# Where the low part of x is made, and when the expert units are loaded, in a convolution-and-experts kernel

## The reference

```
k = conv(x, w1, padding 6, dilation 2);  k = relu(k + b1)
k = relu(batch_norm(conv(k, w2) + b2));  attn = softmax(k, axis=1)
out = sum over p of patch_p(x) * attn[:, p]          # 49 taps
x = x + out
t = t + experts(ln(t)),  top 2 of 8 experts, weights from a softmax over mean(t) @ Wr
```

## Time and profile before

| | us |
|---|---|
| median of 3 runs | 980.85 (979.34 to 983.98) |
| the profiled execution | 980.27, of which the span of the trace is 978.5 |
| PE busy | 909.7 (93%) |
| DVE busy | 699.5 (71%) |
| ACT busy | 528.8 (54%) |
| POOL busy | 141.8 (14%) |
| 16 unit loads xs<-in_ew, 512 KB each | median 4.3 from issue to landing |

### The profile page before, as it was taken

The page is one execution under the profiler, slowest core; times in us unless marked ns, Lnnn a source line. Parts: engine busy times, 40 slices in busy tenths (PEclk is TensorE's granted clock), DMA queues, the critical chain, the costliest instruction groups (busy, mean ns, idle before and its releaser), DMA issues. The chain is left out here.

```text
span 978.5 us, 19546 instructions
## 1 busy us (share of the span) xinstructions
PE 909.7 (93%) x7659; PEld 755.1 (77%) x7659; DVE 699.5 (71%) x1824; ACT 528.8 (54%) x981; POOL 141.8 (14%) x164
## 2 busy tenths in 40 slices
PE   3787999999999969999999947999999999999997
PEld 2776888888888858888999934777777777777776
DVE  3797567477658619836579866878877887788777
ACT  4796343434444211133445438686867777687851
POOL 1100110000010200200113220111221212112122
PEclk9999999999999998989999968999999999999999
DMA  9721311132200144720558446354255335424211
GB/s 215 217 61 52 95 49 50 50 91 62 63 26 25 45 138 131 200 50 2 132 150 220 133 121 164 90 128 96 64 152 110 66 85 159 98 50 98 66 33 49
DMA packets 134826, 95.01 MB, mean 97 GB/s; under 512 B 63579, under 2 KB 129516, under 8 KB 134636
## 3 DMA queue, kind: packets, MB, share of 16 engines
q1 hardware_dynamic: 134734, 93.77, 37.5%
HBM read 54.91 MB, written 29.40 MB: 86 GB/s over the span
## 5 line engine op out<-in xcount | busy, mean ns | idle before, releaser
L1316 PE MATMUL pM<-V,U 128*128 128x264 f16 (+3 forms) x2352 | 294.6, 283 | 0.0
L1316 PEld LDWEIGHTS pM<-V,U 128*128 128x128 f16 x2352 | 230.5, 99 | 44.6
L1824 ACT ACTIVATE gf<-pH,b1c,sc 128x384 f32<-128x384 f32 x192 | 127.7, 669 | 83.8 <-issue 67.2
L2131 PE MATMUL pH<-xT,w1h 128*128 128x384 f16 x768 | 157.9, 329 | 5.8 <-DMA xT<-xs 3.4
L2145 PE MATMUL pY<-w2h,gh 128*128 128x256 f16 x576 | 157.0, 273 | 0.3 <-DVE w2l L1989 0.3
L2145 PE MATMUL pY<-w2h,gl 128*128 128x256 f16 x576 | 157.0, 273 | 0.0
L2145 PE MATMUL pY<-w2l,gh 128*128 128x256 f16 x576 | 157.0, 273 | 0.0
L1997 DVE SCALAR_TENSOR_TENSOR gl<-gf,sc,gh 128x384 f16<-128x384 f32 x192 | 112.1, 620 | 50.2 <-ACT gh L1815 50.2
L2131 PEld LDWEIGHTS pH<-xT,w1h 128*128 128x128 f16 x768 | 75.0, 99 | 55.6 <-ACT gf L1824 4.8
L1815 ACT ACTIVATE gh<-gf,sc 128x384 f16<-128x384 f32 x192 | 115.4, 616 | 0.0
L775 ACT CAST V<-pV 128x336 f16<-128x336 f32 x96 | 42.0, 437 | 133.3 <-PE pV L1287 133.3
(11 more groups left out here) (252 smaller groups left out, 1357.2 us busy)
## 6 DMA issues: line engine op xcount, KB each, us to landing
xa<-in_xt SPq DMA_DIRECT2D x16, 576.0 KB, 6.4
xs_scratch<-xs SPq DMA_DIRECT2D x16, 576.0 KB, 4.3
tk<-t_scratch SPq DMA_DIRECT2D x24, 384.0 KB, 3.8
out<-o SPq DMA_DIRECT2D x23, 384.0 KB, 2.9
xs<-in_ew SPq DMA_DIRECT2D x16, 512.0 KB, 4.3
U<-xs_scratch SPq DMA_DIRECT2D x16, 480.0 KB, 4.7
V<-in_w1g SPq DMA_DIRECT2D x6, 784.0 KB, 8.4
w1r<-in_ew SPq DMA_DIRECT2D x8, 512.0 KB, 4.3
```

What stands on the lines that cost most here:

```text
L1316: return nc.tensor.matmul(out[:, :, first:end], U[:, k, hi_u, piece, :], V[:, b % 2, hi_v, k, c, :, first + TILES * d:end + TILES * d], st ...
L1824: nc.scalar.activation(gf[:, (JB * m + j) % GBUFS, :], pH[:, (JB * m + j) % HBUFS, 0:CN], ACT.Gelu, bias=b1c[:, j // FB, j % FB:j % FB + 1 ...
L2131: last = nc.tensor.matmul(pH[:, (JB * m + j) % HBUFS, 0:CN], w[:, k, c, f * P:(f + 1) * P], xT[:, s, x, c, :], start=(i == 0), stop=(i == ...
```

## The change

Two edits. The low part of x, a subtraction of 96x1536 elements for each of the 16 images, is no longer VectorE's but GpSimd's, which has it in its program among its reciprocal roots. And SyncE issues the loads of the first three expert units before the store and loads of the norm's numbers, the attention maps and the spread table, the other fourteen where all stood; the slots of the last batch in which VectorE takes units begin at 1 instead of 0, and slots 7 and 8 have three units each instead of two.

```
-STAGES, UNITS_SLOT = 3, {0: 1, 1: 2, 2: 2, 3: 2, 4: 2, 5: 2, 6: 2, 7: 2, 8: 2}
+STAGES, UNITS_SLOT = 3, {1: 1, 2: 2, 3: 2, 4: 2, 5: 2, 6: 2, 7: 3, 8: 3}
@@ block.sync, behind the loops over the batches
+            def load_units(units):
+                for u in units:
+                    if u >= STAGES:
+                        sp.wait_ge(unit_taken, u - STAGES + 1)
+                    src, dst = unit(u)
+                    sp.dma_start(dst, src).then_inc(unit_loaded[u % STAGES], 16)
+
+            sp.wait_ge(v_turned, V_TURNS * IMGS)
+            for s in range(2):
+                sp.wait_ge(xs_stored[s], 16 * IMGS // 2)
+            load_units(range(STAGES))
             sp.wait_ge(ln_taken, 2)
             sp.dma_start(ln_d.rearrange("w (r p) -> r w p", p=TT), ln_rows).then_inc(ln_stored, 16)
...
             sp.wait_ge(m_ready, NP * (B - 1) + G_FREE)
             sp.dma_start(G[:, :, :], spread_d).then_inc(g_loaded, 16)
-            for s in range(2):
-                sp.wait_ge(xs_stored[s], 16 * IMGS // 2)
-            sp.wait_ge(v_turned, V_TURNS * IMGS)
-            for u in range(UNITS):
-                if u >= STAGES:
-                    sp.wait_ge(unit_taken, u - STAGES + 1)
-                src, dst = unit(u)
-                sp.dma_start(dst, src).then_inc(unit_loaded[u % STAGES], 16)
+            load_units(range(STAGES, UNITS))
@@ block.gpsimd
+            def x_low(n):
+                pool.wait_ge(xhi_split, n + 1)
+                nc.gpsimd.tensor_tensor(xs[:, n % 2, :, 1, :], xa[:, n % XBUFS], xs[:, n % 2, :, 0, :],
+                                        ALU.subtract).then_inc(xlo_split, 1)
+
             rsqrt(0)
             rsqrt(1)
+            x_low(0)
             rsqrt(2)
             pool.wait_ge(bn_step, 1)
             pool.wait_ge(size_step, 6)
             nc.gpsimd.tensor_tensor(bnp[:, 6:7], bnp[:, 5:6], mhalf[0:TAPS, 0:1], ALU.pow).then_inc(bn_rstd, 1)
+            x_low(1)
             for n in range(3, IMGS):
                 rsqrt(n)
+                if n <= BI:
+                    x_low(n - 1)
+                if n >= BI:
+                    x_low(n)
@@ block.vector
-            def x_low(n):
-                dve.wait_ge(xhi_split, n + 1)
-                tt(xs[:, n % 2, :, 1, :], xa[:, n % XBUFS], xs[:, n % 2, :, 0, :], ALU.subtract).then_inc(xlo_split, 1)
-
...
                     u_low(U_PAIR * pair + j)
-                    if pair + j == 0:
-                        x_low(0)
...
-                x_low(pair + 1)
...
-                    if k in SPLIT_SLOT and BI * (b + 1) + SPLIT_SLOT[k] < IMGS:
-                        x_low(BI * (b + 1) + SPLIT_SLOT[k])
```

## The result

The changed kernel takes 983.77 us in the median (980.57 to 990.81) beside 979.10 us of the kernel before: ratio 1.0042, interval [1.0026, 1.0058], 4.1 us more (2.5 to 5.7).

What follows compares the result with a forecast made beforehand. Setup was taken as bound by engines handing work round, the convolution by TensorE. Loads and table -8.8, setup +8.2, convolution +2.4 gave +1.8 on 980.3, so 982.1 us, range 974 to 990.

Steps and rivals of the forecast that it cites:

- The stall: Last batch: TensorE idles 8.62 us before logits while VectorE awaits the first expert unit; early loads save 11.0 us.
- The table: Last batch, slots 7 and 8: three units each delay VectorE's spread subtraction; TensorE's fourth spread waits, +2.2 us (0 to 3.3).
- GpSimd's operation: Each image's low-part subtraction, 96x1536: 3.45 us on GpSimd, range 2.9 to 4.0, against VectorE's 1.75.
- Convolution: Images 5, 6, 7, 10 and 14: GpSimd's low part comes late for TensorE's turn, +2.4 us in all.
- Image 0: Setup: GpSimd finishes the low part later, so TensorE's turn starts at 27.3 instead of 25.59, +1.7 us.
- Image 1: Setup: GpSimd's low part stops VectorE's tap-table multiply, delaying TensorE by 0.7 us; 3.4 if L1158 is caught instead.
- Images 2 and 3: Setup: GpSimd's low part stops VectorE's tap-table multiply, for which TensorE waits; +2.5 and +2.2 us.
- Rival 1: Setup: GpSimd does not stop the tap-table multiply; sum -5.5, 974.8 us. Chance 18%, 22% with a faster GpSimd operation.
- Clock: Setup, images 2 and 3: idle TensorE may drop to its lower clock, 1.6 us each; one taken, +1.6 (0 to 3.2).
- Image 4: Setup: GpSimd delivers the low part at 96.2, ahead of TensorE's former start at 96.80; -0.5 us.
- Rival 2: Low parts everywhere: mixed form slower on GpSimd, 990.1 us at 4.0 us each; chance 20%, 28% with image 1's other collision.
- Rival 3: Last batch: loads not early enough or late slots swallow the gain, first part gives about nothing; 991 us, chance 4%.

Runs made afterwards that it cites:

- pool_plus_1us: Changed kernel plus a 6-column GpSimd power operation ahead of the low parts of images 5 to 15; 1.0139 of the kernel before, +13.6 us.
- behind_bn: Changed kernel, but GpSimd starts image 1's low part only after the six steps of bn_scales; 1.0018 of the kernel before, +1.8 us.
- behind_taps: Changed kernel, but GpSimd starts the low parts of images 2 and 3 only after their pair's tap table is scaled; 0.9960 of the kernel before, -3.9 us.
- low_only: Changed kernel with unit loads and slot table put back as before, low parts still on GpSimd; 1.0097 of the kernel before, +9.5 us.
- table_in_psum: Changed kernel with the tap table copied once to PSUM and read there by VectorE's multiply; 0.9959 of the kernel before, -4.0 us.
- loads_only: Changed kernel with every low part back on VectorE, early loads and new slot table kept; 0.9932 of the kernel before, -6.7 us.

## Why the prediction was right in its sum and wrong in its steps

The forecast of 982.1 us and "within 0.5%" held: +1.8 forecast, +4.1 measured, though the interval reaches to 0.58% and the loss itself is clear of zero. That it held is in part luck: the setup lost 13.2 us instead of 8.2, and the convolution nothing instead of 2.4.

- **The stall** (-11.0). Right: between the same two logits -11.2 us in the trace, VectorE's wait for the first unit gone, TensorE 30.00 of 30 us busy.
- **The table** (+2.2). Right place and mechanism, three takes ahead of the fourth spread; the size was low. In the trace of the changed kernel the wait is 1.66 us, and 3.4 are lost over the spreads; the pairs of variants have 2.4 to 3.9. The 21 matmuls behind the wait took 4.01 us instead of 2.60, a low clock that the term left out.
- **GpSimd's operation** (3.45 us). 3.10: (3096 - 195)/1530 = 1.90 ns a column, not 2.13. The mixed form is cheaper than the f32 one. By the Trainium skill, GPSIMD Engine Reference, section 3.1, the estimate was 3.4 us; it is for f32, and for this form the measurement decides against both.
- **Convolution** (+2.4). Wrong, from that term: 0.08 + 3.10 fits into the 3.27 us with 0.1 to spare. `pool_plus_1us` shows that the mechanism was right: by its waits, little more than 0.1 us added to the operation would have begun to cost.
- **Image 0** (+1.7). Right: 1.4 us in every trace with GpSimd there, in line with 3.10 - 1.75. Another 0.4 us lie ahead of it and are the kernel's start. The matmuls behind it ran at the low clock (3.18 us for eight), 1.2 us more than before up to the mark of image 1; but variants with image 0 on VectorE have up to 2.4 more, so this is not shown to be the change's doing.
- **Image 1** (+0.7). This step failed. I left the other collision, L1158's, out of the sum and gave it 8%, together with low clocks at both later images; both occurred. It cost 2.9 us instead of 0.7; `behind_bn`, without it, is 2.8 us shorter in that stretch of the trace and 2.3 in the ratio. When an outcome hangs on which of two operations starts first within 0.1 us, a chance near one half was due: of the five traces with this order left open it was caught in two (the changed kernel, `behind_taps`) and free in three (`low_only`, `table_in_psum`, `pool_plus_1us`). The collision that I did forecast here, GpSimd's end against the multiply, is real but smaller: 0.58 us for 0.34 in `low_only`.
- **Images 2 and 3** (+2.5, +2.2). Rival 1 is out: the multiply is stopped, 2.37 us instead of 0.34. The direct price was 2.03 each.
- **Clock** (+1.6, one of two falls). Too low: both came, 1.57 us at image 2 and 2.3 at image 3. Low stretches of the clock ahead of the first convolution matmul sum to 21.7 us after, 5.1 before. At images 0, 1, 2 and 3 the matmuls behind a wait of 2.5 to 2.9 us ran at the low level; at image 1 they had done so before the change too. The stretches between the waits are longer by 1.2, 0.3, 1.6 and 2.3 us behind images 0 to 3, 5.3 in all, and for the two multiplies' part, 3.9, this agrees with the ratios (8.0 - 4.1).
- **Image 4** (-0.5). -0.8.

Setup in the trace: 0.4 for the start + 1.4 + 2.9 + 2 x 2.03 + 5.3 for these stretches - 0.8 = 13.2, but for rounding, against 8.2. Rival 2's mechanism is out, at 3.10 us; what it named beside it (image 1's collision and cold starts at both later images, +6.1) is what happened, and the sum stayed at +4.1 mainly because the convolution cost nothing. Rival 3 is out: `loads_only` gains 6.7 us.

The Trainium skill, SBUF — State Buffer, section "SBUF: two separate sides", has the pair of ports shared by VectorE and GpSimd as an exclusive lock for the whole instruction, held by whichever starts first. The traces agree: 2.37 us for 0.34, 3.14 for 0.24, GpSimd's 4.05 for 3.10 where VectorE was first, and 0.24 where VectorE was 0.08 us ahead. What tells the two scalings from the one-column operations that ran free, no run here separates.

## What to carry to other kernels

Before moving an operation to GpSimd, list what VectorE does from SBUF during it on the way to the bottleneck engine: the price here was less the operation's length (1.4 us at image 0, nothing in the convolution) than that list, each stopped entry lengthened to the end of GpSimd's instruction, and then the low clock of the TensorE work behind the wait. A wait that orders GpSimd behind VectorE's few short critical operations, or a PSUM operand for them, removed 8 to 10 us here. And change one thing at a time: the early loads were worth 9 to 11 us, and the new table that came with them gave back 2 to 4. Before you trust 1 or 2 us at a mark in one trace, look at the same mark in another trace of the same kernel; here they differed by up to 2.9.

## What the runs showed of the hardware that I had not expected

- A VectorE scaling of 49x49 elements waits for a whole 3.1 us GpSimd instruction, and whether it does is settled by less than 0.1 us: 0.08 us ahead it took 0.24 us, 0.01 ahead 3.14. Four one-column operations in the middle of such an instruction took 0.15 to 0.17 us, as always.
- The same multiply reading its tensor from PSUM runs beside GpSimd in 0.45 us (0.34 from SBUF when free).
- The hold works both ways, and GpSimd can then take the ports between two dependent VectorE operations (4.05 us, then 2.97 for a 24-column one).
- A subtraction of f32 and f16 into f16 on GpSimd costs 1.90 ns a column, less than the 2.13 of its f32 addition.
- After a TensorE wait of 2.7 us, eight matmuls that take 1.78 us took 2.3 to 3.4 in every trace, half speed for part or all of them. After 0.69 us they took 1.78 each time. After 2.1 us, at image 1, anything from 1.78 to 3.35, so the length of the wait alone does not settle it.
